# Cross attention in a decoder layer: dividing the probabilities before they are turned, and adding the outputs by channel

## The chip, the cores and the metric

One core of a Trainium2 chip runs the whole program. The time is device microseconds of one execution. The kernel before took 2195.38 us (median of three runs, 2195.28 to 2197.44). The engines are TensorE (PE in the rows; PEld is its weight loading), VectorE (DVE), ScalarE (ACT), GpSimd (POOL) and SyncE (SP), which issues the transfers. Each runs its own instructions in order, and they wait for one another by semaphores.

## The reference, cut to what matters

Three parts follow one another, each added to its input and normalized: a gated long convolution with its multilayer part, the attention, and a low rank feed-forward part. The change lies in the attention, over 16 batches of 512 tokens with 16 heads of 16 channels. The context has 64 tokens:

```python
y = jnp.einsum('bhqk,bhkd->bhqd', jax.nn.softmax(att, axis=-1), v)          # causal self attention
qc = _heads(x @ Wcq + bcq)
kc = _heads(cross_input @ Wck + bck)
vc = _heads(cross_input @ Wcv + bcv)
attc = jnp.einsum('bhqd,bhkd->bhqk', qc, kc) * scale
y = y + jnp.einsum('bhqk,bhkd->bhqd', jax.nn.softmax(attc, axis=-1), vc)    # cross attention
y = y.transpose(0, 2, 1, 3).reshape(x.shape[0], T, C)
return y @ Wp + bp
```

All of it is in float32; products are of split numbers (a high and a low part, three products) or of float32 as it is.

## The kernel before

The attention stage (`attend`) runs one step for each batch, and two steps ahead of the first. A step has 44 slots. In each slot TensorE does up to four things in this order: the weights of one unit of self attention (`weights`, 40 units, each then exponentiated by ScalarE into `pt` and masked on its diagonal by GpSimd, the "cut"), the jobs that the table `SLOTS` names for the slot, the value products of a chunk two slots behind its last unit (`outputs`, in slots 5, 11, 15, 21, 25, 31, 35 and 41), the turning of a head group's output (`turn_out`, in slots 13, 23, 33 and 43), and one piece of the next batch's scores (`scores`), whose maxima VectorE takes (L1743). Two banks hold scores and two hold weights, so that TensorE can be at most two slots ahead of VectorE's maxima and of ScalarE's exponentials. The jobs share three PSUM banks, `ps_j`, in turn.

Jobs are named by a letter and a number: c is the cross query, kc and vc are the context's keys and values, v the values, t the turning of the input, q and k the self attention's queries and keys, n the turned maxima, y the turning of the output, p the output projection. Each step works on several batches: q, k and t two ahead, c, s, w, o and r one ahead, y and p one behind. The cross attention is four kinds of job:

- s (8 jobs, L1666 and L1669 on VectorE): scores of 128 tokens by 8 heads x 64 context tokens. VectorE takes the maximum of each head and writes the scores less the maximum into `sd`. There is one `sd` for each quarter of the tokens, so s4 waits until w3 has read it.
- w (8 jobs, L1346, L1480): a head pair's shifted scores of all 512 tokens are turned (four transpositions of 128x128), and ScalarE takes their exponential into `ptc`.
- o (4 jobs, L1352, L1483): two head pairs' values times `ptc`. The values carry a column of ones for each head, which gives the sum of its exponentials, and are 32 columns a head wide (`VW`), so one pair makes 64 output rows. ScalarE copies the result to `sc`.
- r (4 jobs, L1357, L1677, L1679): `sc` is turned back to tokens by channels (four transpositions), and VectorE divides by the sum and writes into `y`.

`divide` then does the same for the self attention's output and adds it to `y` (L1704, L1706, L1710). The jobs y0 and y1 of the next step turn `y` to channels by tokens (L1361), and it is split in a high part (ScalarE, L1487) and a low part (VectorE, L1683) for the projection.

Other work of GpSimd in a step: `low_part` (L1559) in the slots of q and k (9, 11, 17, 19), `context_keys` (L1573) in slots 3 to 6, the layer norm's root (`ln_root`, L1579 to L1585) in slot 16 and the residual addition (L1589) in slot 37. The order of all of it is written out by hand in the code of each engine's `step` and in the table.

## Time and profile before

| | |
|---|---|
| median of three runs | 2195.38 us |
| profiled execution | 2197.36 us |
| its span | 2195.6 us |
| TensorE busy over the span | 1985.4 us, 90% |
| VectorE | 1468.2 us, 67% |
| ScalarE | 1222.3 us, 56% |
| GpSimd | 883.2 us, 40% |
| mean granted clock of TensorE | 0.965 of full speed |

The page has these shares, and a strip of forty slices. In that strip the attention stage is the long middle part, where TensorE is at nine tenths or more in every slice and its clock is at full speed. The timeline gives the instructions of one engine in order of time, with the idle time ahead of each and who ended it. Views by stretches give the busy time of each engine between two moments.

### The profile page before, as it was taken

To read this page: it belongs to the slowest core of one execution; us is meant where nothing else is said; L and a number is where in the kernel's file an instruction comes from. 1 tells how busy PE (TensorE), PEld (TensorE's weight loads), DVE (VectorE), ACT (ScalarE), POOL (GpSimd) and SP (SyncE) were. 2 spreads that over 40 slices of the span, in tenths; PEclk is the share of its full clock that TensorE was granted. 3 is DMA by queue.
4 is the path that set the end of the run, shared out by engine and by line. 5 is a ranking of instruction groups with operands and counts; after the bars stand their busy time and mean duration, and the time that the engine had idled before them with its cause. 6 is when DMAs were issued, how large, how long until landed. Compare 5 with 4: busy or idle time off the path is not lost. (4 is left out here: it accounts for less than half of the span.)

```text
span 2195.6 us, 39396 instructions
## 1 busy us (share of the span) xinstructions
PE 1985.4 (90%) x12897; PEld 1348.4 (61%) x12960; DVE 1468.2 (67%) x2652; ACT 1222.3 (56%) x2425; POOL 883.2 (40%) x1336
## 2 busy tenths in 40 slices
PE   6786949999999868999999999999999999968997
PEld 4665337888888755566566665566655665535554
DVE  6898634555555427777778777777777787724776
ACT  6775535555555423665656656565656556645554
POOL 3443615555555431334333434344333433332222
PEclk9999969999999979999999999999999999978999
DMA  3343121211122244343443344342443334112221
GB/s 116 123 149 125 44 77 68 77 68 69 67 73 76 78 106 91 77 106 72 104 105 85 79 93 103 92 103 64 109 103 80 90 81 94 43 39 66 78 87 66
DMA packets 104787, 188.10 MB, mean 86 GB/s; under 512 B 27961, under 2 KB 78137, under 8 KB 98489
## 3 DMA queue, kind: packets, MB, share of 16 engines
q1 hardware_dynamic: 104632, 186.13, 31.7%
q8 instruction: 86, 1.41, 0.3%
q14 instruction: 69, 0.56, 0.1%
HBM read 110.23 MB, written 58.79 MB: 77 GB/s over the span
## 5 line engine op out<-in xcount | busy, mean ns | idle before, releaser
L1516 ACT ACTIVATE at_pt<-at_ps_w 128x512 f32<-128x512 f32 x640 | 377.8, 598 | 232.8 <-PE at_ps_w L1392 232.7
L1743 DVE TENSOR_REDUCE at_mneg<-at_ps_s 128x1 f32<-128x384 f32 (+3 forms) x704 | 437.3, 636 | 94.9 <-PE at_ps_s L1381 87.3
L1606 POOL TENSOR_SCALAR_AFFINE_SELECT at_pt<-at_pt 128x256 f32<-128x256 f32 (+1 forms) x640 | 233.5, 368 | 576.3 <-ACT at_pt L1516 573.8
L1380 PE MATMUL at_ps_s<-at_ks,at_qs 96*128 96x128 bf16 (+3 forms) x1024 | 259.4, 306 | 25.0 <-DVE at_mneg L1743 22.7
L1392 PE MATMUL at_ps_w<-at_qs,at_ks 97*128 97x512 bf16 (+3 forms) x1024 | 244.3, 301 | 9.0 <-ACT at_pt L1516 5.0
L1380 PEld LDWEIGHTS at_ps_s<-at_ks,at_qs 96*128 96x128 bf16 x1024 | 86.2, 99 | 215.1 <-DVE at_mneg L1743 140.5
L895 POOL TENSOR_TENSOR ml_m_lo<-ml_m,ml_m_hi 128x512 fp32r<-128x512 f32 x80 | 115.9, 1450 | 181.0 <-ACT ml_m_hi L801 180.7
L1408 PE MATMUL at_ps_o<-at_pt,at_val 128*32 128x512 f32 (+3 forms) x2048 | 169.1, 449 | 9.7 <-POOL at_pt L1606 9.5
L1381 PE MATMUL at_ps_s<-at_mask,at_ident 128*128 128x128 bf16 (+1 forms) x641 | 149.4, 233 | 0.0
L834 ACT ACTIVATE ml_gl<-ml_ps_g 128x512 f32<-128x512 f32 x96 | 56.7, 591 | 153.8 <-PE ml_ps_u L127 150.0
L1392 PEld LDWEIGHTS at_ps_w<-at_qs,at_ks 97*128 97x128 bf16 x1024 | 88.3, 98 | 62.9 <-ACT at_pt L1516 14.8
L1559 POOL TENSOR_TENSOR at_parts<-at_rest,at_parts 128x512 bf16<-128x512 f32 x64 | 74.4, 1163 | 130.4 <-ACT at_parts L1493 130.4
L125 PE MATMUL ml_ps_o<-gw_wd,ml_m_hi 128*128 128x256 f32 x320 | 91.8, 287 | 12.8 <-POOL ml_rest L900 7.0
L1022 DVE TENSOR_TENSOR ml_m<-ml_gl,ml_ps_u 128x512 f32<-128x512 f32 x80 | 54.7, 683 | 72.7 <-POOL ml_rest L900 42.0
L381 ACT ACTIVATE pj_zc<-pj_ps_z,pj_tb,pj_tap 128x512 f32<-128x512 f32 x96 | 74.5, 780 | 47.0 <-PE pj_ps_z L127 46.9
L1666 DVE TENSOR_REDUCE at_mcneg<-at_ps_j 128x8 f32<-128x512 f32 x128 | 87.7, 685 | 17.3 <-PE at_ps_j L127 17.2
L1911 ACT ACTIVATE ff_hid<-ff_ps_h,fw_bias 128x512 f32<-128x512 f32 x128 | 79.3, 687 | 35.5 <-PE ff_ps_h L1843 34.2
L1669 DVE TENSOR_TENSOR at_sd<-at_ps_j,at_mcneg 128x512 f32<-128x512 f32 x128 | 88.6, 692 | 13.5 <-DVE at_mcneg L1666 0.5
L1002 DVE TENSOR_TENSOR ml_r<-ml_ps_o,ml_xy 128x1024 f32<-128x1024 f32 x16 | 19.6, 1225 | 116.3 <-PE ml_ps_o L943 116.3
L125 PE MATMUL at_ps_j<-at_x_hi,ea_w_hi 128*128 128x512 f32 x192 | 90.8, 473 | 6.7 <-DVE at_rest L1647 5.2
L125 PE MATMUL pj_ps_z<-pj_x_hi,pj_w_hi 128*128 128x512 f32 x192 | 80.2, 418 | 15.2 <-DVE pj_x_lo L483 15.2
L1408 PEld LDWEIGHTS at_ps_o<-at_pt,at_val 128*32 128x32 f32 x2048 | 51.9, 111 | 66.3 <-issue 44.3
(255 smaller groups left out, 5582.3 us busy)
## 6 DMA issues: line engine op xcount, KB each, us to landing
parts_d<-at_parts SPq DMA_DIRECT2D x64, 384.0 KB, 2.5
at_ks<-parts_d SPq DMA_DIRECT2D x192, 128.0 KB, 7.8
at_qs<-parts_d SPq DMA_DIRECT2D x32, 384.0 KB, 5.7
pj_xin<-in_x SPq DMA_DIRECT2D x16, 512.0 KB, 5.3
gate_d<-pj_zc SPq DMA_DIRECT2D x16, 512.0 KB, 2.7
xv_all<-pj_turned_xv SPq DMA_DIRECT2D x16, 512.0 KB, 4.2
ml_turned_y<-xv_all SPq DMA_DIRECT2D x16, 512.0 KB, 3.4
ml_x<-gate_d SPq DMA_DIRECT2D x16, 512.0 KB, 4.3
```

Of the source, the lines that this page charges most:

```text
L125: pe.matmul(out, lh, rh, start=first and k == 0, stop=False)
L895: pool.tensor_tensor(m_lo[slot(k, par)][:], m[k % 2][:], m_hi[slot(k, par)][:].bitcast(F32), ALU.subtract).then_inc(m_low, 1)
L1380: pe.matmul(out[:, i, :], qs[par][0:ROWS, h, toks], ks[par][0:ROWS, h, 0:(qt + 1) * P], start=i == 0, stop=False)
L1381: pe.matmul(out[:, :, toks], ident16[:], mask16[:, 0:count, :], start=False, stop=True).then_inc(scored, 1)
L1392: mm = pe.matmul(bank[:, at0:at0 + T - kt * P], ks[par][:, h, kt * P:(kt + 1) * P], qs[par][:, h, kt * P:T], start=True, stop=True)
L1408: mm = pe.matmul(ps_o[j * VW:(j + 1) * VW, kt * P:T], val[par][:, kt, g * HG + j, :], pt[unit % RING][:, at0:at0 + T - kt * P], start=kt = ...
L1516: act.activation(pt[u % RING][:], ps_w[u % 2][:], ACT.Exp, scale=SCALE).then_inc(exped, 1)
L1606: pool.affine_select(out=diag, in_=diag, compare_op=ALU.is_ge, fill=0.0, base=0, pattern=pattern, channel_multiplier=-1).then_inc(cut, 1)
L1666: dve.tensor_reduce(top, scored_c, AX_X, ALU.max, negate=True).then_inc(mc_set, 1)
L1669: dve.tensor_tensor(sd[qt][:].rearrange("p (e s) -> p e s", s=CL), scored_c, top.unsqueeze(2).to_broadcast([P, HE, CL]), ALU.add).then_inc ...
L1743: dve.tensor_reduce(mneg[:, g, h0 % HG:h0 % HG + count, qt], view_score(ps_s[s % 2], qt, count), AX_X, ALU.max, negate=True).then_inc(maxe ...
L1911: act.activation(hid[k % RING][:], ps_h[k % RING][:], ACT.Gelu_apprx_tanh, bias=bias1[:, k:k + 1]).then_inc(gelu_done, 1)
```

## The change

The probabilities are divided while they still lie as tokens by context. Two slots after an s job ScalarE takes the exponential of `sd` in place. Four slots after it VectorE sums the exponentials of each head and takes the reciprocal (`cross_share`), and GpSimd multiplies `sd` by it (`cross_scale`). The w jobs turn finished probabilities, and ScalarE only copies them. An o job now takes four head pairs with 32 columns each, so two o jobs do what four did, and their output is by channel: there are no r jobs, and no `sc`. ScalarE keeps the outputs in `yc`. `y` holds self attention alone; `divide` has no addition. The jobs y turn it, VectorE adds the turned bank to `yc`, ScalarE makes the high part and GpSimd the low part. In the table vc is in slot 18 and the w jobs are in slots 22 to 25 and 39 to 42, the s jobs of the second half in 26 to 32. Ahead of the stage, SyncE clears the seven semaphores of the long convolution at the end of the multilayer part.

```diff
-SLOTS = """c0 c1 kc v0,n3 v1 t0 t1 y0 y1 q0 s0 k0 s1 p0 s2 p1 s3,n0 q1 w0 k1 vc w1 w2 w3,o0 n1,s4 r0 o1 s5 r1
-           s6 - s7 - - w4 w5 w6,o2 w7 r2,o3 n2 r3 - - -""".split()
+SLOTS = """c0 c1 kc v0,n3 v1 t0 t1 y0 y1 q0 s0 k0 s1 p0 s2 p1 s3,n0 q1 vc k1 - - w0 w1 n1,w2 w3 s4 - s5 o0 s6 - s7
+           - - - - - - n2,w4 w5 w6 w7 o1""".split()
...
+            for semaphore in spent:
+                sp.sem_clear(semaphore)
...
                 elif kind == "w":
                     k, own = i // QT, slice(i % QT * P, (i % QT + 1) * P)
-                    cleared([f"s{QT * k + q}" for q in range(QT)], name, b)
+                    pe.wait_ge(cross_scaled, KT * QT * b + QT * (k + 1))
...
-                    for a in range(2):
-                        mm = pe.matmul(bank[a * 2 * VW:(a + 1) * 2 * VW, :], valc[:, 2 * i + a].rearrange("p a v -> p (a v)"),
-                                       ptc[:, (2 * i + a) % (HE // 2), :], start=True, stop=True)
-                elif kind == "r":
-                    cleared([f"o{i}"], name, b)
-                    for q in range(QT):
-                        mm = pe.transpose(bank[:, q * P:(q + 1) * P], sc[:, q * P:(q + 1) * P], ident[:])
+                    for a in range(QT):
+                        mm = pe.matmul(bank[a * 2 * HD:(a + 1) * 2 * HD, :], valc[:, QT * i + a].rearrange("p a v -> p (a v)"),
+                                       ptc[:, a, :], start=True, stop=True)
...
-                    act.activation(ptc[:, i % (HE // 2), :], bank[:], ACT.Exp, scale=SCALE).then_inc(clear(name, b)[0], 1)
+                    act.activation(ptc[:, i % QT, :], bank[:], ACT.Copy).then_inc(clear(name, b)[0], 1)
...
+            def cross_exp(name, b):
+                act.wait_ge(*clear(name, b))
+                qt = int(name[1]) % QT
+                act.activation(sd[qt][:], sd[qt][:], ACT.Exp, scale=SCALE).then_inc(cross_exped, 1)
...
+                    for name in crossed(b, u, 2):
+                        cross_exp(name, b + 1)
...
+            def cross_scale(name, b):
+                number = KT * QT * b + int(name[1])
+                pool.wait_ge(cross_shared, number + 1)
+                qt = int(name[1]) % QT
+                scores = sd[qt][:].rearrange("p (e s) -> p e s", s=CL)
+                pool.tensor_tensor(scores, scores, shares[int(name[1]) % 2][:].unsqueeze(2).to_broadcast([P, HE, CL]),
+                                   ALU.mult).then_inc(cross_scaled, 1)
+
+            def output_low(name, b, npar):
+                i = int(name[1])
+                pool.wait_ge(y_high, 2 * b + i + 1)
+                pool.tensor_tensor(yt_lo[:, i, :], yc[npar][:, i, :], yt_hi[:, i, :].bitcast(F32), ALU.subtract).then_inc(y_low, 1)
...
-                elif kind == "r":
-                    dve.wait_ge(front_ready, at(name, b))
-                    src = bank[:].rearrange("p (q h v) -> p q h v", h=HG, v=VW)
...
-                    dve.reciprocal(rdenc[:], src[:, :, :, HD]).then_inc(rdenc_set, 1)
-                    dve.wait_ge(rdenc_set, NG * b + i + 1)
-                    dve.tensor_tensor(y[npar][:, :, i * HG:(i + 1) * HG, :], src[:, :, :, 0:HD],
-                                      rdenc[:].unsqueeze(3).to_broadcast([P, QT, HG, HD]), ALU.mult).then_inc(done, 1)
                 elif kind == "y":
-                    dve.wait_ge(y_high, 2 * b + i + 1)
-                    dve.tensor_tensor(yt_lo[:, i, :], bank[:], yt_hi[:, i, :].bitcast(F32), ALU.subtract).then_inc(done, 1)
+                    dve.wait_ge(tail_ready, at(name, b))
+                    dve.wait_ge(*clear("o%d" % i, b))
+                    dve.tensor_tensor(yc[npar][:, i, :], bank[:], yc[npar][:, i, :], ALU.add).then_inc(done, 1)
...
+            def cross_share(name, b):
+                i = int(name[1])
+                number = KT * QT * b + i
+                dve.wait_ge(cross_exped, number + 1)
+                sums = mcneg[:, i % QT, i // QT * HE:(i // QT + 1) * HE]
+                dve.tensor_reduce(sums, sd[i % QT][:].rearrange("p (e s) -> p e s", s=CL), AX_X, ALU.add).then_inc(cross_summed, 1)
+                dve.wait_ge(cross_summed, number + 1)
+                wait(dve, cross_scaled, number - 1)
+                dve.reciprocal(shares[i % 2][:], sums).then_inc(cross_shared, 1)
...
-                own = y[par][:, :, g * HG:(g + 1) * HG, :]
-                dve.tensor_tensor(own, own, ys[:], ALU.add).then_inc(y_added, 1)
+                dve.tensor_tensor(y[:, :, g * HG:(g + 1) * HG, :], src[:, :, :, 0:HD],
+                                  rden[:].unsqueeze(3).to_broadcast([P, QT, HG, HD]), ALU.mult).then_inc(y_set, 1)
...
+                    for name in crossed(b, u, 4):
+                        cross_share(name, b + 1)
```

The helper `crossed(b, u, later)` names the s jobs of the slot `later` slots back. On VectorE and on GpSimd its work stands at the end of the slot: on VectorE behind the slot's maximum, on GpSimd behind the slot's cut and low part and ahead of context keys, root and residual.

GpSimd, slots 13 to 20 of a steady step, before. AFFINE_SELECT is the cut of a unit, `at_parts` the low part, the four rows from `at_lnv` to `at_mv` the layer norm's root:

```order
L1606 AFFINE_SELECT at_pt<-at_pt 128x2x128 x3
L1579 TENSOR_SCALAR at_lnv<-at_mv 128x4
L1580 TENSOR_SCALAR at_mv<-at_mv 128x4
L1583 TENSOR_TENSOR at_lnr<-at_lnv,at_mhalf 128x4
L1585 TENSOR_TENSOR at_mv<-at_mv,at_lnr 128x4
L1606 AFFINE_SELECT at_pt<-at_pt 128x2x128
L1559 TENSOR_TENSOR at_parts<-at_rest,at_parts 128x512
L1606 AFFINE_SELECT at_pt<-at_pt 128x2x128 x2
L1559 TENSOR_TENSOR at_parts<-at_rest,at_parts 128x512
```

And now, from the multiplication for s1 in slot 16 on:

```order
L1602 TENSOR_TENSOR at_sd<-at_sd,at_shares 128x512
L1589 TENSOR_SCALAR at_lnv<-at_mv 128x4
L1590 TENSOR_SCALAR at_mv<-at_mv 128x4
L1593 TENSOR_TENSOR at_lnr<-at_lnv,at_mhalf 128x4
L1595 TENSOR_TENSOR at_mv<-at_mv,at_lnr 128x4
L1629 AFFINE_SELECT at_pt<-at_pt 128x2x128
L1569 TENSOR_TENSOR at_parts<-at_rest,at_parts 128x512
L1629 AFFINE_SELECT at_pt<-at_pt 128x2x128
L1602 TENSOR_TENSOR at_sd<-at_sd,at_shares 128x512
L1629 AFFINE_SELECT at_pt<-at_pt 128x2x128
L1569 TENSOR_TENSOR at_parts<-at_rest,at_parts 128x512
L1629 AFFINE_SELECT at_pt<-at_pt 128x128
```

A multiplication of `sd` stands ahead of the root and between the cuts of units 18 and 19; the value product of slot 21 needs the cut of unit 19.

VectorE, from slot 16's s3 on, before. `at_mneg` are the maxima of self attention, `at_rest` the work of q1 and k1:

```order
L1666 TENSOR_REDUCE at_mcneg<-at_ps_j 128x8
L1669 TENSOR_TENSOR at_sd<-at_ps_j,at_mcneg 128x512
L1743 TENSOR_REDUCE at_mneg<-at_ps_s 128x1
L1647 SCALAR_TENSOR_TENSOR at_rest<-at_ps_j,ea_bias,at_parts 128x512
L1743 TENSOR_REDUCE at_mneg<-at_ps_s 128x1 x2
L1647 SCALAR_TENSOR_TENSOR at_rest<-at_ps_j,ea_bias,at_parts 128x512
L1743 TENSOR_REDUCE at_mneg<-at_ps_s 128x1
```

And now:

```order
L1696 TENSOR_REDUCE at_mcneg<-at_ps_j 128x8
L1699 TENSOR_TENSOR at_sd<-at_ps_j,at_mcneg 128x512
L1773 TENSOR_REDUCE at_mneg<-at_ps_s 128x1
L1726 TENSOR_REDUCE at_mcneg<-at_sd 128x8
L1729 RECIPROCAL at_shares<-at_mcneg 128x8
L1676 SCALAR_TENSOR_TENSOR at_rest<-at_ps_j,ea_bias,at_parts 128x512
L1773 TENSOR_REDUCE at_mneg<-at_ps_s 128x1
L1670 TENSOR_TENSOR at_valc<-at_ps_j,ea_brow 64x8x16 x2
L1773 TENSOR_REDUCE at_mneg<-at_ps_s 128x1
L1726 TENSOR_REDUCE at_mcneg<-at_sd 128x8
L1729 RECIPROCAL at_shares<-at_mcneg 128x8
L1676 SCALAR_TENSOR_TENSOR at_rest<-at_ps_j,ea_bias,at_parts 128x512
```

The sums and reciprocals of s1 and s2 stand behind the maxima of slots 16 and 18, and the context's values (vc) have moved up between them.

TensorE, slot 23, before: `at_sd` is a w job, `at_ptc` an o job, `at_so` turn_out:

```order
L1346 MATMUL at_ps_j<-ea_ident,at_sd 128x128 x4
L1352 MATMUL at_ps_j<-at_ptc,at_valc 64x512 x2
L1416 MATMUL at_ps_o<-ea_ident,at_so 128x128 x4
L1380 MATMUL at_ps_s<-at_ks,at_qs 128x256 x2
L1381 MATMUL at_ps_s<-at_mask,at_ident 128x2x128
```

And now:

```order
L1356 MATMUL at_ps_j<-ea_ident,at_sd 128x128 x4
L1422 MATMUL at_ps_o<-ea_ident,at_so 128x128 x4
L1386 MATMUL at_ps_s<-at_ks,at_qs 128x256 x2
L1387 MATMUL at_ps_s<-at_mask,at_ident 128x2x128
```

These are the rows of slot 23. The o job has left it, and its w job is now w1, where it was w3.

## Rows read from the trace of the kernel before

**Rows 1.** Stretches: us, then busy us and count by engine, TensorE's clock.

```profile
1216.20:1286.40 70.20, 67.84 (x513) 43.32 (x516) 54.31 (x107) 42.12 (x81) 27.31 (x54) 1.00 0.40 92
...
1100.00:1900.00 800.00, 770.61 (x5809) 490.08 (x5854) 620.02 (x1216) 477.98 (x919) 307.12 (x616) 1.00 0.38 89
```

**Rows 2.** TensorE's timeline, an o job and an r job: start, us, instruction.

```profile
1207.29 1.08 PE L1352 MATMUL at_ps_j<-at_ptc,at_valc 128*64 128x512 f32 x4
1208.30 0.34 PE L1380 MATMUL at_ps_s<-at_ks,at_qs 96*128 96x384 bf16 x1
...
1209.64 0.60 PE L1357 MATMUL at_ps_j<-ea_ident,at_sc 128*128 128x128 f32 x4
1210.17 1.08 PE L1352 MATMUL at_ps_j<-at_ptc,at_valc 128*64 128x512 f32 x4
```

**Rows 3.** TensorE's timeline from out3 to slot 26.

```profile
1252.94 1.50 PE L1408 MATMUL at_ps_o<-at_pt,at_val 128*32 128x384 f32 x24
...
1254.99 0.61 PE L1346 MATMUL at_ps_j<-ea_ident,at_sd 128*128 128x128 f32 x4
1255.43 0.39 PE L1380 MATMUL at_ps_s<-at_ks,at_qs 96*128 96x128 bf16 x4
...
1259.63 0.50 PE L125 MATMUL at_ps_j<-at_km_hi,at_cq_hi 128*128 128x512 f32 x1 [0.67 <-ACT at_ptc L1480]
...
1260.44 0.40 PE L1380 MATMUL at_ps_s<-at_ks,at_qs 96*128 96x256 bf16 x2
...
1261.54 1.07 PE L1408 MATMUL at_ps_o<-at_pt,at_val 128*32 128x512 f32 x8
...
1262.77 0.38 PE L1392 MATMUL at_ps_w<-at_qs,at_ks 97*128 97x384 bf16 x2
```

**Rows 4.** VectorE's timeline, slots 12 to 18.

```profile
1237.97 0.69 DVE L1666 TENSOR_REDUCE at_mcneg<-at_ps_j 128x8 f32<-128x512 f32 x1 [0.23 <-PE at_ps_j L127]
1238.76 0.69 DVE L1669 TENSOR_TENSOR at_sd<-at_ps_j,at_mcneg 128x512 f32<-128x512 f32 x1
...
1240.85 0.42 DVE L1706 TENSOR_TENSOR at_ys<-at_ps_o,at_rden 128x256 f32<-128x256 f32 x1
1241.31 0.42 DVE L1710 TENSOR_TENSOR at_y<-at_y,at_ys 128x256 f32<-128x256 f32 x1
...
1248.38 0.55 DVE L1743 TENSOR_REDUCE at_mneg<-at_ps_s 128x1 f32<-128x384 f32 x1
1248.84 0.74 DVE L1647 SCALAR_TENSOR_TENSOR at_rest<-at_ps_j,ea_bias,at_parts 128x512 f32<-128x512 f32 x1
1249.50 1.15 DVE L1743 TENSOR_REDUCE at_mneg<-at_ps_s 128x1 f32<-128x384 f32 x2
```

**Rows 5.** GpSimd's timeline, slots 16 to 18.

```profile
1246.81 0.20 POOL L1579 TENSOR_SCALAR at_lnv<-at_mv 128x4 f32<-128x4 f32 x1 [0.53 <-DVE at_mv L1698]
...
1248.62 0.41 POOL L1606 TENSOR_SCALAR_AFFINE_SELECT at_pt<-at_pt 128x256 f32<-128x256 f32 x1
1250.33 1.16 POOL L1559 TENSOR_TENSOR at_parts<-at_rest,at_parts 128x512 bf16<-128x512 f32 x1 [1.31 <-ACT at_parts L1493]
1251.44 0.84 POOL L1606 TENSOR_SCALAR_AFFINE_SELECT at_pt<-at_pt 128x256 f32<-128x256 f32 x2
```

**Rows 6.** Line L1573 by tile: count, ns min/median/max, first and last start.

```profile
L1573 POOL TENSOR_TENSOR at_km_hi<-at_kc_hi,ea_heads x32: 1043/1044/1047, 807.6 to 1856.9; 128x512 fp32r<-128x512 f32 x32
```

**Rows 7.** GpSimd's timeline at the end of the step.

```profile
1280.27 2.36 POOL L1589 TENSOR_TENSOR at_r<-at_r,ea_brow 128x1024 f32<-128x1024 f32 x1
1282.58 0.78 POOL L1606 TENSOR_SCALAR_AFFINE_SELECT at_pt<-at_pt 128x256 f32<-128x256 f32 x2
```

**Rows 8.** TensorE's timeline there: the value product of slot 41.

```profile
1283.41 1.50 PE L1408 MATMUL at_ps_o<-at_pt,at_val 128*32 128x384 f32 x24 [0.28 <-POOL at_pt L1606]
```

**Rows 9.** Stretches of step -1, columns as in rows 1.

```profile
848.00:859.40 11.40, 7.11 (x39) 3.49 (x41) 10.69 (x21) 0.60 (x1) 0.00 (x0) 1.00 0.61 88
859.40:862.90 3.50, 3.50 (x18) 2.58 (x17) 2.69 (x5) 0.60 (x1) 0.00 (x0) 0.51 0.00 0
```

More of the change, by code:

```diff
@@ L1123, in attend @@
         ptc = n.sb("ptc", [P, HE // 2, T])
[L1124 removed]
+        valc = n.sb("valc", [P, HE, 2, HD])
         so = n.sb("so", [P, T])
[L1126 to L1129 removed]
+        shares = [n.sb(f"shares{i}", [P, HE]) for i in range(2)]
+        rden = n.sb("rden", [P, QT, HG])
+        y = n.sb("y", [P, QT, H, HD])
+        yc = [n.sb(f"yc{i}", [P, KT, T]) for i in range(2)]
         yt_hi, yt_lo = n.sb("yt_hi", [P, KT, T], F32R), n.sb("yt_lo", [P, KT, T], F32R)
@@ L1160, in attend @@
         PARS = early.pars
-        CONSTS = 9
+        CONSTS = 7
         def at(job, b):
@@ L1185, in slots, with crossed @@
                 yield u, [j for j in names if shown(j, b)]
+        def crossed(b, u, later):
+            names = SLOTS[u - later] if u >= later else []
+            return [j for j in names if j[0] == "s" and shown(j, b)]
         def before(job, b):
@@ L1529, in _ @@
             for name in TAIL:
-                job(name, B - 1)
+                job(name, B - 1, 1)
             for q in range(QT):
@@ L1617, in _ @@
             over_steps(pool, step)
+            for name in ("y0", "y1"):
+                output_low(name, B - 1, 1)
             ln_root(B - 1)
```

77 lines of the change are left out of this document (37 added, 40 removed).

## The prediction

> **What bounds the kernel now.** I read the page's busy shares first, then the stage by stretches, then the timeline of one steady step, engine by engine. The change touches the attention stage alone (and adds seven semaphore clears on SyncE at the end of the stage before it). That stage runs one step per batch, 14 of them alike. The one that I read, from the start of its c0 job to the next one's, is 1216.2 to 1286.4, 70.2 us; in it TensorE is busy 67.8 us, VectorE 54.3, ScalarE 42.1, GpSimd 27.3, at full clock, as in all 800 us around it [rows 1]. So TensorE bounds the step, and what leaves its stream should be gained, as long as nobody is late for it. TensorE is in order, and the reader is to see in rows 3 to 5 and 7 how near the others already come: the transposition w3 is waited for through its exponential (0.67 us before s4 [rows 3]), and the last value product of the step waits 0.28 us for GpSimd's masking, which stands behind a 2.36 us addition there [rows 7, 8].
>
> I call slots by their number: 44 in a step, about 1.6 us each. "out3" is the value product of slot 21, "out7" that of slot 41.
>
> **TensorE's saving.** Gone are four r jobs (0.53 us each from 1209.64 to 1210.17 [rows 2]) and half of the eight o pairs' time: an o job took 1.01 us for two heads' pairs (1207.29 to 1208.30 [rows 2]), with 64 output columns each. The new one has four products of 32 columns. The value product of slot 25 has that form, four of 32 columns and 512 elements, and takes 1.07 us from its first start to its last end [rows 3], where the o job of two took 1.08 [rows 2]. So two o jobs now cost 2.0 for 4.0. Together 2.1 + 2.0 = 4.1 us a step.
>
> **VectorE's change.** Gone: four divisions r (reciprocal and multiplication), four additions L1710. An instruction starts some 0.08 before the end of an independent one (1248.38 + 0.55 against 1248.84, 0.74 before 1249.50) and some 0.1 after one that it needs (1237.97 + 0.69 against 1238.76 [rows 4]). So the addition takes 0.46 off (1240.85 to 1241.31 [rows 4]), an r about 0.6. Added: eight shares, each a sum over 128x512 (0.79 until its reciprocal may start, as L1666 to L1669) and a reciprocal of 8 columns, for which I take 0.17 from its larger sister (0.25 less the overlap; between 0.1 and 0.25): 0.96 each. Net 7.7 - 1.8 - 2.5 = +3.4 us. Throughput is not exceeded (57.7 of 66). Where it stands is what counts.
>
> **ScalarE.** Four copies of sc go, two copies o and eight exponentials come, some 0.5 each: +3 us on 42, two slots ahead of need. I cost it at nothing; the cover is its 28 us of idle time in a step.
>
> **GpSimd.** Added: eight multiplications of 128x512. No such row exists. The nearest has two inputs, one broadcast: 1.044 us [rows 6]; the addition of rows 7 does 1024 elements in 2.36, so 1.18 for 512. I take 1.10. Also two subtractions y at the same price, in slots 7 and 8, where no value product is near; nothing. The trouble is that GpSimd runs in order, and the masking ("cut") of each unit, which the value products wait for, now queues behind a multiplication that itself waits for VectorE.
> The Trainium skill ("GPSIMD Engine Reference", Engine selection) holds against two-input work on GpSimd that it is about twice as slow as VectorE. Against VectorE's 0.69 the rows above say 1.5 to 1.7 times; by the rule a multiplication would be 1.38 and the step 0.8 us longer, since three stand on the path below, 12 us in all. The rows decide.
>
> **First place: out3.** VectorE is without a pause from 1237.97 to 1250.65, the end of slot 18, in the trace (13 rows more lie between those shown [rows 4]). Its slot 16 ended with the reduction before 1248.84. Add s0's share (0.96), take off the addition (0.46), and add s1's share until its end (0.79 + 0.25): 1250.38. From there GpSimd is one queue: handover 0.15 (an estimate; 0.05 between rows 7 and 8), multiplication 1.10, the layer norm's root 1.81 (1246.81 to 1248.62), cut 0.41, the low part 1.11 (1250.33 to 1251.44 [rows 5]), cut 0.41, multiplication 1.10, the cut of unit 19 0.41, handover 0.05: out3 starts at 1256.93 where it started at 1252.94 [rows 3]. **+4.0**. TensorE, with w0 and w1 gone from ahead of it, stands idle for most of 4 us.
>
> **From out3 to slot 26.** Before: 1252.94 to 1262.77, 9.83 us [rows 3]. Gone: o0 1.01, s4 with its wait 0.67 + 0.81, r0 0.45 (0.53 less a change of tile shape that stays, some 0.08). Added: two transpositions of 0.44 (1254.99 to 1255.43), and w0's wait for s3's multiplication: GpSimd needs 1.11 + 0.31 + 1.10 + 0.05 after the cut, TensorE 2.05, so 0.5. Sum 8.24: slot 26 starts at 1265.2, **+2.4** against before.
>
> **Second place: slots 26 to 39.** TensorE has only four s, one o and the small work here, some 13 us; VectorE is the longer. It starts 1.2 after the slot does (s4 0.81: 1259.63 to 1260.44 [rows 3]; 0.2 each, as estimates, for the unit's scores ahead of it and for the end of the last product) and then has, until s7's share is done: four s of 1.40 (0.79 + 0.61), four shares of 0.96 (the last with 0.25 whole), one division 0.62, four reductions of 384 at 0.46, seven of 512 at 0.60 = 16.2 us: 1282.6. GpSimd then: 0.15, multiplication 1.10, cut 0.41, the residual addition 2.31 (1280.27 to 1282.58 [rows 7]), two cuts 0.82, 0.05: out7 at 1287.4, before 1283.41 [rows 8]. Meanwhile w4, w5 and w6 fit in.
>
> **To the end of the step.** Before 2.99 (1283.41 to 1286.4 [rows 1, 8]). Now w7 (0.44), o1 (1.01) and o1's wait for the copy of w7 (0.60 of ScalarE and two handovers less a score of 0.3, so 0.57) are in it: 5.01. The step ends at 1292.4: **+6.0 us**, in which TensorE's 4.1 are already counted.
>
> **The clock.** Before, TensorE is at full clock in the steady stretch [rows 1]. Where it was busy 7.11 of 11.40 us, its clock then stood at 0.51 for 3.5 us [rows 9], that is the lower of its two levels, 1.2 GHz. A pause of 4 us at out3, with smaller ones ahead of it, leaves TensorE idler than that. I expect one such fall a step, right before out3, w0 to w3 and out4, where TensorE is the bound: 3.4 us of work at half speed lose 1.7 us. Bounds: nothing, and two falls, 3.4.
> The Trainium skill ("TensorE: Matmul & The Clock Gate", Part 1) has the gate go to half rate after an idle stretch; rows 9 agree. Without it the sum would be the second case below.
>
> **Sum.** 14 steady steps (batches 1 to 14): 14 x 6.0 = 84.0. Step 0 has no layer norm root: 6.0 - 1.8 = 4.2. Step -1 is VectorE's (10.69 us busy of 11.40 [rows 9]); it gains up to 7.7 - 2.5 = 5.2 of its work, between 0 and that I take 4. The last step has no cross attention: 0. Clock 14 x 1.7 = 23.8. The clears: seven SyncE instructions beside a block's end, under 1 us, nothing. Together +116.0 on the span of 2195.6 = 2311.6, and 1.8 around it (2197.36 - 2195.6): 2313.4. The profiled execution lies 0.1% above the median of 2195.38, so I leave it at that: **2313 us**.
>
> **Rivals.**
> (a) The forecast: waits at GpSimd's queue, and the clock falls with them. Chance 0.50.
> (b) The waits without the falls: 2290. For it: the value products and transpositions around the pauses are dense. Against: rows 9. Chance 0.23.
> (c) The waits are half as long (+3 us a step, few falls), about 2240. VectorE's chain would have to be some 3 us looser at both places, for instance if sums from SBUF are quicker than from PSUM. Against: 12.7 us without a gap in rows 4's stretch. Chance 0.15.
> (d) The other side: TensorE stays the bound and the 4.1 us are gained in 15 steps, 2197.4 - 61.5 = 2136. Mechanism: cut 19 and s7's share come in time. It decides where out3's cut is ready by 1252.1 (its old start less w0 and w1's transpositions), that is if the 6.55 us of GpSimd's queue were under 1.7. No row of it can shrink so. It needs VectorE to run ahead as well. Chance 0.06.
> (e) Two falls a step, or multiplications of 1.4 us: 2340 to 2365. Chance 0.06.
> That the outputs by channel do not save TensorE time at all (32 columns cost as 64) would add 2.0 a step only where TensorE bounds; it is within (a).
>
> **How the numbers follow.** 2313 is that of (a); its own range, with 0.5 to 1.5 falls and 5 to 7 us a step, is 2285 to 2335. For 8 in 10 I take in (b), the upper part of (c) and the lower of (e): 2250 to 2350. A difference of 0.2% (4.4 us) is what a measurement tells. Faster: (d), 0.06. Within: the edge between (c) and (d), 0.02. Slower: 0.92.
>
> **What would show it.** Right: a steady step of 76 to 79 us; TensorE's longest waits on L1414 (out3, out6, out7) for GpSimd's cut, and on L1356 (w0, w4) for the multiplication; granted clock under 1.00 in the steady stretch; GpSimd without a pause from s1's multiplication to cut 20. o jobs of four products in 1.0 us. Wrong: no wait over 1 us at L1414, or a step under 70 us. The sum is wrong in size if the multiplication is not 1.05 to 1.2, or a share not about 0.96.

## The result, and the profile after

The changed kernel takes **2301.01 us** (median of 4 runs, 2300.68 to 2303.87), the kernel before 2195.33 (4 runs on the same chip): ratio **1.048** (95% interval 1.046 to 1.050), slower. The forecast was 2313 in a range of 2250 to 2350. The profiled execution took 2301.33, with a span of 2299.6, 104.0 us more than before's.

Counted between the starts of the first and the last residual addition of the stage, 15 steps apart, a step of after takes 74.43 us on average and one of before 68.26 (first and last start are 938.7 and 2055.2, and 929.4 and 1953.3 before). Among batches 1 to 14 alone, from c0 to c0, it is 76.53 against 70.22 (948.45 to 1943.32 and 937.34 to 1850.21, 13 intervals each): **+6.3 us a step**. Step -1 gave 6.3 more, step 0 5.3, and the time from the last c0 to the end of the program 10.9, in which the last full step's 6.3 are contained.

Stretches of after, columns as in [rows 1]: a steady step, two parts of it, and the long stretch.

```profile
1330.50:1407.00 76.50, 66.33 (x499) 42.01 (x502) 56.90 (x113) 45.87 (x88) 37.33 (x64) 0.98 0.37 85
...
1367.50:1370.70 3.20, 0.09 (x5) 0.03 (x4) 2.86 (x6) 2.38 (x6) 3.20 (x6) 1.00 0.27 94
1370.70:1374.20 3.50, 3.50 (x27) 1.45 (x28) 0.11 (x1) 1.13 (x3) 2.56 (x4) 0.51 0.42 140
...
1100.00:1900.00 800.00, 700.38 (x5188) 445.88 (x5229) 593.12 (x1160) 478.77 (x911) 390.71 (x669) 0.96 0.36 83
```

The reader is to compare the last row with the last of [rows 1]: TensorE was busy 771 of 800 us and is now busy 700, though part of it ran at a lower clock; no other engine is near its limit (VectorE 593, GpSimd 391). Nobody became the bound as a total. The time is in pauses, and the rows in the middle are one of them: 3.2 us in which TensorE did 0.09 us of work while GpSimd worked without a gap, and behind it 3.5 us at 0.51 of the clock, the lower of the two levels.

TensorE's timeline of that step, whose c0 starts at 1330.51 and the next one's at 1406.44 (start, us, instruction, in brackets its idle time and whom it waited for), beside [rows 3, 8]:

```profile
1370.68 2.73 PE L1414 MATMUL at_ps_o<-at_pt,at_val 128*32 128x384 f32 x24 [3.11 <-POOL at_pt L1629]
...
1379.64 0.38 PE L1398 MATMUL at_ps_w<-at_qs,at_ks 97*128 97x384 bf16 x2
...
1393.48 1.06 PE L1414 MATMUL at_ps_o<-at_pt,at_val 128*32 128x512 f32 x8 [1.48 <-POOL at_pt L1629]
...
1398.28 0.63 PE L1356 MATMUL at_ps_j<-ea_ident,at_sd 128*128 128x128 f32 x4 [1.32 <-POOL at_sd L1602]
...
1401.59 1.50 PE L1414 MATMUL at_ps_o<-at_pt,at_val 128*32 128x384 f32 x24 [1.29 <-POOL at_pt L1629]
...
1404.65 1.07 PE L1362 MATMUL at_ps_j<-at_ptc,at_valc 128*32 128x512 f32 x8 [0.46 <-issue]
...
1406.41 0.38 PE L1398 MATMUL at_ps_w<-at_qs,at_ks 97*128 97x512 bf16 x1
```

Four waits for GpSimd stand where before had one of 0.28 us: out3 (3.11), out6 (1.48), w4 (1.32) and out7 (1.29). The first row also shows the clock: 24 products that took 1.50 us in [rows 3] take 2.73 here.

This step is one of the two shortest of steps 1 to 13 (75.9 us, the average is 76.5), and in its clock it isn't typical. Read stretch by stretch, after has 24 stretches of 3.5 us at the lower level in these 13 steps, 6.4 us a step; before has none in them. Only this step and one other have a single one. Eleven have two: in six of them the two adjoin, from some 2 us ahead of out3 to 5 us behind it, and in five the second comes 24 to 27 us later, at out6 or w4. A whole step of the first kind, and pieces out of the two stretches of a step of the second kind:

```profile
1100.41:1177.05 76.64, 66.47 (x498) 42.09 (x500) 56.37 (x111) 45.89 (x87) 37.34 (x64) 0.96 0.37 85
...
1217.25:1220.50 3.25, 2.93 (x25) 1.12 (x26) 0.15 (x1) 0.81 (x3) 2.90 (x5) 0.50 0.49 165
1241.25:1244.50 3.25, 3.25 (x17) 2.09 (x17) 2.37 (x6) 1.51 (x3) 1.94 (x4) 0.50 0.00 0
```

GpSimd's timeline ahead of out3 and ahead of out7, beside [rows 5, 7]:

```profile
1364.42 1.05 POOL L1602 TENSOR_TENSOR at_sd<-at_sd,at_shares 128x512 f32<-128x512 f32 x1 [3.75 <-DVE at_shares L1729]
1365.55 0.20 POOL L1589 TENSOR_SCALAR at_lnv<-at_mv 128x4 f32<-128x4 f32 x1
...
1367.36 0.41 POOL L1629 TENSOR_SCALAR_AFFINE_SELECT at_pt<-at_pt 128x256 f32<-128x256 f32 x1
1367.74 1.16 POOL L1569 TENSOR_TENSOR at_parts<-at_rest,at_parts 128x512 bf16<-128x512 f32 x1
1368.84 0.41 POOL L1629 TENSOR_SCALAR_AFFINE_SELECT at_pt<-at_pt 128x256 f32<-128x256 f32 x1
1369.22 1.04 POOL L1602 TENSOR_TENSOR at_sd<-at_sd,at_shares 128x512 f32<-128x512 f32 x1
1370.21 0.41 POOL L1629 TENSOR_SCALAR_AFFINE_SELECT at_pt<-at_pt 128x256 f32<-128x256 f32 x1
...
1397.09 1.04 POOL L1602 TENSOR_TENSOR at_sd<-at_sd,at_shares 128x512 f32<-128x512 f32 x1 [0.57 <-ACT at_pt L1528]
...
1398.46 2.35 POOL L1612 TENSOR_TENSOR at_r<-at_r,ea_brow 128x1024 f32<-128x1024 f32 x1
1400.77 0.77 POOL L1629 TENSOR_SCALAR_AFFINE_SELECT at_pt<-at_pt 128x256 f32<-128x256 f32 x2
```

The first row is s1's multiplication, which had to wait 3.75 us for VectorE's share. From there to the cut of unit 19 (1370.21 to 1370.62) GpSimd has no gap: multiplication, root, cut, low part, cut, multiplication, cut. Below the second "..." is the queue ahead of out7, with the residual addition in the middle.

VectorE's timeline where s1's share is made, beside [rows 4]:

```profile
1363.42 0.68 DVE L1726 TENSOR_REDUCE at_mcneg<-at_sd 128x8 f32<-128x512 f32 x1
1364.13 0.20 DVE L1729 RECIPROCAL at_shares<-at_mcneg 128x8 f32<-128x8 f32 x1
1364.25 0.71 DVE L1676 SCALAR_TENSOR_TENSOR at_rest<-at_ps_j,ea_bias,at_parts 128x512 f32<-128x512 f32 x1
```

And the lines of the page that hold most of the waits: count, busy us, mean ns, idle time before them and its releaser.

```profile
L1414 PE MATMUL at_ps_o<-at_pt,at_val 128*32 128x512 f32 (+3 forms) x2048 | 186.3, 488 | 93.0 <-POOL at_pt L1629 92.8
L1602 POOL TENSOR_TENSOR at_sd<-at_sd,at_shares 128x512 f32<-128x512 f32 x128 | 133.7, 1045 | 214.3 <-DVE at_shares L1729 208.6
L1356 PE MATMUL at_ps_j<-ea_ident,at_sd 128*128 128x128 f32 x512 | 83.9, 291 | 18.9 <-POOL at_sd L1602 18.9
```

In these, 93 us of TensorE's idle time is the value products' wait for GpSimd's cut and 19 us the transpositions' wait for the multiplication: 112 us over 16 steps, 7.0 each. The other part is the clock: 6.4 us a step at half speed make TensorE's own work 3.2 us longer. 7.0, less the 0.3 that before had, and 3.2 make 9.9, and with the 4.1 that left TensorE's stream some 5.8 of the 6.3.

### The profile page after: what moved, and what is told of

Same layout as the page of the kernel before. It is cut to its first block and busy times, and to the rows that moved or that the text cites. A ratio compares the mean times of both kernels' runs of the same rounds, so it can differ in the third digit from the quotient of the medians.

```text
span 2299.6 us, 39230 instructions
## 1 busy us (share of the span) xinstructions
PE 1963.2 (85%) x12641; PEld 1327.7 (58%) x12704; DVE 1502.5 (65%) x2716; ACT 1281.4 (56%) x2521; POOL 1043.2 (45%) x1494
## 5 line engine op out<-in xcount | busy, mean ns | idle before, releaser
L1528 ACT ACTIVATE at_pt<-at_ps_w 128x512 f32<-128x512 f32 x640 | 371.9, 593 | 196.1 <-PE at_ps_w L1398 190.7
L1386 PE MATMUL at_ps_s<-at_ks,at_qs 96*128 96x128 bf16 (+3 forms) x1024 | 270.2, 316 | 38.5 <-DVE at_mneg L1773 34.1
L1414 PE MATMUL at_ps_o<-at_pt,at_val 128*32 128x512 f32 (+3 forms) x2048 | 186.3, 488 | 93.0 <-POOL at_pt L1629 92.8
L1398 PE MATMUL at_ps_w<-at_qs,at_ks 97*128 97x512 bf16 (+3 forms) x1024 | 249.7, 306 | 14.7 <-ACT at_pt L1528 10.3
L1602 POOL TENSOR_TENSOR at_sd<-at_sd,at_shares 128x512 f32<-128x512 f32 x128 | 133.7, 1045 | 214.3 <-DVE at_shares L1729 208.6
L1414 PEld LDWEIGHTS at_ps_o<-at_pt,at_val 128*32 128x32 f32 x2048 | 56.9, 119 | 157.5 <-POOL at_pt L1629 112.9
L1398 PEld LDWEIGHTS at_ps_w<-at_qs,at_ks 97*128 97x128 bf16 x1024 | 90.7, 101 | 75.2 <-issue 20.1
L1356 PE MATMUL at_ps_j<-ea_ident,at_sd 128*128 128x128 f32 x512 | 83.9, 291 | 18.9 <-POOL at_sd L1602 18.9
L1569 POOL TENSOR_TENSOR at_parts<-at_rest,at_parts 128x512 bf16<-128x512 f32 x64 | 74.4, 1162 | 53.6 <-ACT at_parts L1505 53.5
```

What stands on the lines that cost most here:

```text
L1356: mm = pe.transpose(bank[:, q * P:(q + 1) * P], sd[q][:, own], ident[:])
L1386: pe.matmul(out[:, i, :], qs[par][0:ROWS, h, toks], ks[par][0:ROWS, h, 0:(qt + 1) * P], start=i == 0, stop=False)
L1398: mm = pe.matmul(bank[:, at0:at0 + T - kt * P], ks[par][:, h, kt * P:(kt + 1) * P], qs[par][:, h, kt * P:T], start=True, stop=True)
L1414: mm = pe.matmul(ps_o[j * VW:(j + 1) * VW, kt * P:T], val[par][:, kt, g * HG + j, :], pt[unit % RING][:, at0:at0 + T - kt * P], start=kt = ...
L1528: act.activation(pt[u % RING][:], ps_w[u % 2][:], ACT.Exp, scale=SCALE).then_inc(exped, 1)
L1602: pool.tensor_tensor(scores, scores, shares[int(name[1]) % 2][:].unsqueeze(2).to_broadcast([P, HE, CL]), ALU.mult).then_inc(cross_scaled, 1)
```

## The experiments

All ratios are against the kernel before, run on the same chip at the same time; 4 runs each where nothing else is said. The theory A of each expectation is the prediction's: GpSimd's queue, and VectorE ahead of it, make TensorE wait at two places, and the clock falls there. Theories C and D, in e4 and e5, are about what the falls cost.

**e1, the root out of the queue ahead of out3.** The layer norm's root (slot 16) is issued in slot 21, and ScalarE's four normalizations come five slots later with it (in slots 24 to 27).

```
+ROOT_SLOT = 21
-                    if 0 <= u - P1_SLOT - 4 < QT and shown("p1", b):
-                        layernorm(b - 1, u - P1_SLOT - 4)
+                    if 0 <= u - ROOT_SLOT - 3 < QT and shown("p1", b):
+                        layernorm(b - 1, u - ROOT_SLOT - 3)
-                    if u == P1_SLOT + 1 and shown("p1", b):
+                    if u == ROOT_SLOT and shown("p1", b):
```

> The changed kernel with one thing moved: the layer norm's root on GpSimd from slot 16 (behind the multiplication for s1) to slot 21 (behind that slot's cut), and ScalarE's four normalizations with it, to slots 24 to 27. Nothing else. Theory A (GpSimd's queue sets the start of out3): the root's 1.81 us leave the queue between s1's multiplication and cut 19, TensorE's wait at out3 falls from 3.1 us to about 1.3 to 1.6, each of 14 steps is 1.5 to 1.8 us shorter, total 2270 to 2280. Rival B (VectorE's own chain sets it, and GpSimd's cut is only the last that is seen): the share for s2 is late too, the root filled a time in which GpSimd would wait anyway, total 2296 to 2301.

**e2, the residual addition out of the queue ahead of out7.**

```
-                    if u == NU - 3 and back(b):
+                    if u == NU - 1 and back(b):
```

> The changed kernel with GpSimd's residual addition moved from slot 37 (ahead of the cuts 38 and 39) to slot 39, behind its cut. Nothing else. Theory A: cut 39 comes 2.3 us earlier, out7 waits no longer (1.29 us in the trace) and o1 follows; a step is 1.3 to 2.0 us shorter, total 2270 to 2282. Rival B (w4 to w7, which wait for the last multiplication, set the end of the step): at most 0.3 us a step, total 2296 or more.

**e3, both.** The edits of e1 and e2.

> Both moves together: root to slot 21 and residual addition to slot 39. Theory A: two separate places on one chain, so the gains add up: 2240 to 2258, with still some 1.5 us of waits at out3, out6 and w4 each step, and a result that stays above the kernel before (2195). Rival B: the second place absorbs what the first gives back, total no lower than the better of the two alone, some 2270.

Measured: e1 2277.47 us (ratio 1.037, 1.035 to 1.039), e2 2279.44 (1.038, 1.037 to 1.040), e3 2255.65 (1.028, 1.026 to 1.031). So 23.5, 21.6 and 45.4 us against after: each inside A's range, and additive. Two jobs that the change did not touch, 1.81 and 2.31 us long, were worth 1.7 and 1.5 us in each of 14 steps (the total by 14, with what it changed in the clock) because of where they stood. The two places are two separate causes, and neither hides behind the other. TensorE's waits for the cut within 1100 to 1900 us (line, releaser, us in all, times, longest), of after, e1, e2 and e3:

```profile
PE at_ps_o L1414 <- POOL at_pt L1629: 57.5, 29, 3.1
```

```profile
PE at_ps_o L1415 <- POOL at_pt L1630: 43.9, 30, 1.6
```

```profile
PE at_ps_o L1414 <- POOL at_pt L1629: 48.8, 21, 3.1
```

```profile
PE at_ps_o L1415 <- POOL at_pt L1630: 33.7, 22, 1.6
```

The longest wait is halved by e1 and untouched by e2, as it should be if 3.1 is out3's; in e2 it is the number of waits that shrinks, from 29 to 21.

**e4, TensorE kept busy ahead of out3.** Ten products are added whose results nobody reads, to see what the fallen clock costs by itself.

```
+                    if back(b) and u in (21,) and shown("c0", b):
+                        pe.wait_ge(exped, NU * b + u)
+                        for _ in range(10):
+                            pe.matmul(ps_w[(u + 1) % 2][:], ident16[:], mask16[:]...)
                     outputs(...)
```

> The changed kernel with ten further products of 512 columns (bfloat16, about 2.2 us at full clock) on TensorE right ahead of out3 in each step that has cross attention, into a weight bank that is free then. They lie in the pause of 3.1 us. Theory C (the pauses cost a fall of the clock on top of themselves): out3 takes 1.5 us again instead of 2.7, half-speed stretches at that place go, and the total falls by 10 to 25 us, to 2276 to 2291. Rival D (the half-speed stretches lie where TensorE is not the bound, or the falls come from other pauses): total 2299 to 2315, since part of the added work is not hidden.

Measured: 2335.41 us (1.064, 1.062 to 1.066), in neither range. TensorE's timeline says why:

```profile
1383.86 4.02 PE L1440 MATMUL at_ps_w<-at_mask,at_ident 128*128 128x512 bf16 x10 [2.61 <-ACT at_pt L1532]
1387.81 0.95 PE L1414 MATMUL at_ps_o<-at_pt,at_val 128*32 128x384 f32 x11
```

The added products stood in a bank that is free only after ScalarE's exponential of the unit before. So they waited 2.61 us, the pause remained, and they themselves ran at half speed (4.02 us for what takes 2.33 in e5 below) and pushed out3 back. The experiment was misplaced and says nothing of the price that it was made for. It does show that the work behind the pause ran slowly here too, though it was other work.

**e5, the same ten products where nothing has to be waited for,** at the start of slot 21's weights, in the bank that they are about to overwrite.

```
                 wait(pe, exped, NU * b + u - 1)
+                if u == 21 and shown("c0", b):
+                    for _ in range(10):
+                        pe.matmul(bank[:], ident16[:], mask16[:]...)
```

> As the run before with added products, but these ten now stand at the start of slot 21, ahead of its weights, where the bank that they write is free at once; in the last one they waited 2.6 us for an exponential of ScalarE and so filled nothing of the pause. They should start with the pause and fill 2.2 of its 3.1 us. Theory C (the pause costs a fall of the clock on top of itself): the product at out3 takes 1.5 us where it took 2.7, total 2276 to 2291. Rival D (the half-speed stretch costs nothing, or falls elsewhere instead): 2297 to 2306.

Measured: 2283.41 us (1.040, 1.037 to 1.043), in C's range. **With 2.3 us of useless work added to each step the kernel is 17.6 us quicker**, 1.3 us a step over 14 steps. TensorE's timeline, and two whole steps, without and with a fall:

```profile
1359.35 2.33 PE L1398 MATMUL at_ps_w<-at_mask,at_ident 128*128 128x512 bf16 x10
...
1362.84 1.50 PE L1417 MATMUL at_ps_o<-at_pt,at_val 128*32 128x384 f32 x24 [0.94 <-POOL at_pt L1632]
...
1365.32 0.63 PE L1356 MATMUL at_ps_j<-ea_ident,at_sd 128*128 128x128 f32 x4 [0.38 <-POOL at_sd L1605]
```

```profile
1247.82:1322.67 74.85, 66.69 (x511) 41.83 (x510) 56.39 (x111) 45.82 (x87) 37.26 (x64) 1.00 0.37 87
1322.67:1397.82 75.15, 68.27 (x511) 42.97 (x510) 56.39 (x111) 45.81 (x87) 37.24 (x64) 0.98 0.37 86
```

Out3 is back at 1.50 us and the mean clock from 1100 to 1900 us at 0.99 (0.96 in after). It starts where it started in after, 40.2 us into the step, so nothing of the gain comes from ahead of it. The Trainium skill ("TensorE: Matmul & The Clock Gate", Part 1) names idleness ahead as what brings the gate down; this pair of kernels agrees: the only edit puts work into the pause, and out3 runs at full speed again.

The 1.3 us are not the whole price, since e5 still has a stretch at half speed in nine of steps 1 to 13, each at w4. A step with one takes 75.1 us. Of the four without one, two take 74.9 and two 75.2, these with another wait in them. After's average is 76.5, so its falls cost some 1.6 us a step together. The price of one depends on where it lies: 0.3 at w4, and 1.1 at out3 with a single stretch (out3 to slot 26 takes 8.96 us in the step shown above, 7.90 in e5).

**e6, the multiplication made small:** it multiplies one of a head's 64 context tokens alone, so the output is not the reference's.

```
-                pool.tensor_tensor(scores, scores, shares[...][:].unsqueeze(2).to_broadcast([P, HE, CL]),
+                pool.tensor_tensor(scores[:, :, 0:1], scores[:, :, 0:1], shares[...][:].unsqueeze(2),
```

> The changed kernel with GpSimd's multiplication done for the first of each head's 64 context tokens alone (8 columns of 512), so its result isn't the reference's; waits and order are kept. Theory A: each multiplication falls from 1.04 to about 0.15 us. Two of them stand ahead of out3, one each ahead of out6, w4 and out7: 3 to 3.6 us a step less and fewer clock falls, total 2238 to 2256. Rival B (VectorE's sums are the price): at most 1 us a step, 2285 or more.

**e7, the sum made small too:** it goes over 4 of the 64 tokens. VectorE and GpSimd then have next to nothing of the change's added work, TensorE has all of its savings.

```
-                dve.tensor_reduce(sums, sd[...].rearrange("p (e s) -> p e s", s=CL), AX_X, ALU.add)
+                dve.tensor_reduce(sums, sd[...].rearrange("p (e s) -> p e s", s=CL)[:, :, 0:4], AX_X, ALU.add)
```

> As the last one, and VectorE's sum also takes only 4 of each head's 64 tokens, so that both added chains are nearly gone, with order and waits kept (not the reference's result). Theory A in its narrow form (all of the loss is the two additions, and what is left is TensorE's stream with 4.1 us less): total 2136 to 2150. Theory A2 (the additions cost 6 us a step, but the table and the root and the residual addition still hold TensorE, so its saving is not gained): 2180 to 2200.

Measured: e6 2233.98 (1.017, 1.014 to 1.020), 67.0 us under after and a little more than A's range gave it; e7 2194.18 (10 runs; 0.9988, 0.9977 to 0.9999), another 39.8, in the range of A2. So the multiplications cost some 4.8 us of each of 14 steps and the sums 2.8, in this order of taking them away, and both together (106.8 us) are the whole loss. The falls are in these figures: of the 24 stretches at half speed in steps 1 to 13, three are left in e6 and four in e7. e6 also has the price of a fall with no other wait to hide in, 1.3 us, from two of its steps:

```profile
1583.76:1655.12 71.36, 64.40 (x501) 40.98 (x500) 56.25 (x111) 45.43 (x87) 30.66 (x64) 1.00 0.39 91
1655.12:1727.76 72.64, 65.70 (x502) 41.40 (x500) 56.26 (x111) 45.54 (x87) 30.66 (x64) 0.98 0.38 89
```

The two are not more than the loss: **with the added work all but gone the kernel stands where it stood before, and most of TensorE's 4.1 us a step are still not gained.** From c0 to c0 a step of e7 takes 69.5 us on average, 0.7 less than before's 70.2, and the ends of the stage are some 6 us longer. Where the rest went is in TensorE's waits within 1100 to 1900 us:

```profile
PE at_ps_o L1414 <- POOL at_pt L1629: 35.2, 36, 1.5
...
PE at_ps_s L1386 <- DVE at_mneg L1773: 13.2, 26, 0.6
```

With the smaller ones these are 54.8 us in 11.5 steps, 4.8 a step, where before had 24.9 us, 2.2 a step. The cut still stands behind the root and the residual addition, and the scores wait for VectorE's reductions (13.2 us, 9.5 in before). The work that TensorE lost had been covering these.

**e8, e3 with share and multiplication one slot earlier** (three behind the scores instead of four).

```
-                    for name in crossed(b, u, 4):
+                    for name in crossed(b, u, 3):
```

(on VectorE and on GpSimd)

> Root in slot 21 and residual addition in slot 39 as before, and VectorE's share and GpSimd's multiplication three slots behind the scores where they were four. The result is the reference's. Theory A: what is waited for at out3, w0 and w4 comes a slot earlier, 1.3 to 1.7 us a step less than with the two moves alone (2255.7), and out6, out7 with it: 2222 to 2238. Rival B (VectorE is full there, so a share done earlier only puts off the maxima that TensorE waits for): 2250 to 2258.

Measured: 2213.63 us (1.008, 1.005 to 1.011), 42.0 less than e3, below the lower end of what was expected. Its waits, same stretch, then the row of that stretch:

```profile
PE at_ps_s L1387 <- DVE at_mneg L1774: 36.8, 56, 1.4
PE at_ps_j L1334 <- DVE at_sd L1700: 16.7, 12, 1.6
PE at_ps_j L1357 <- POOL at_sd L1603: 9.0, 11, 1.1
PE at_ps_o L1415 <- POOL at_pt L1630: 5.7, 11, 1.1
```

```profile
1100.00:1900.00 800.00, 724.85 (x5611) 460.00 (x5610) 635.11 (x1251) 517.78 (x975) 417.49 (x722) 1.00 0.38 88
```

The waits for the cut have fallen from 33.7 to 5.7 us, but they have gone over to VectorE: 53.5 us on its reductions and subtractions (19.0 in e3). With the order of jobs as it is, whichever of the two small engines is relieved, the other is next. All waits together are hardly fewer, 73.4 us for 74.4. What has gone is the half speed: 20 stretches in steps 1 to 13 of e3, one in e8, and the mean clock rises from 0.96 to 1.00 (of TensorE's 800 us, 724.85 are busy, 723.01 in e3: as many, with more done in them).

**e9, another order of jobs.** The root in slot 22, the residual addition behind its cut, the share three slots behind the scores and the multiplication four, and a table with s0 to s3 one or two slots earlier (in 9, 10, 13 and 15) and most of the empty slots strewn between the jobs (the longest row of them is five, six in after).

```
-SLOTS = """c0 c1 kc v0,n3 v1 t0 t1 y0 y1 q0 s0 k0 s1 p0 s2 p1 s3,n0 q1 vc k1 - - w0 w1 n1,w2 w3 s4 - s5 o0 s6 - s7
-           - - - - - - n2,w4 w5 w6 w7 o1""".split()
+SLOTS = """- c0 c1,kc,v0 - v1,t0 t1 - y0 n3 y1,s0 s1,q0 - - s2,k0 - q1,s3 - p0,n0 - p1 - k1,w0 vc w1,w2 - w3,s4,s5 -
+           s6,n1 - - - s7,o0 - - - - - n2 - w4 w5 w6,w7 - o1""".split()
+ROOT_SLOT = 22
-                    for name in crossed(b, u, 4):
+                    for name in crossed(b, u, 3):
```

(the last on VectorE alone)

> The changed kernel with the two moves (root now in slot 22, residual addition in 39), the share three slots and the multiplication four behind the scores, and another table: the s jobs of the first half in slots 9, 10, 13 and 16 with pauses between, those of the second half begun right after w3 in slot 26, y, q and k one to two slots off, so that VectorE's long slots lie between long slots of TensorE. The result is the reference's. Theory A (the form with shares is 4.1 us a step cheaper on TensorE, and only the waits hid it): TensorE is the bound again, a step lasts 65 to 67 us, total 2110 to 2150, under the kernel before. Rival E (the saving on TensorE isn't there, products of 32 columns and the rest cost as much as before): no lower than 2185.

**e10, the kernel before with the two moves of e1 and e2 alone,** in its own lines.

```
+ROOT_SLOT = 21
-                    if u == P1_SLOT + 1 and shown("p1", b):
+                    if u == ROOT_SLOT and shown("p1", b):
-                if u == NU - 3 and back(b):
+                if u == NU - 1 and back(b):
```

> The kernel before, with only the two moves on GpSimd and ScalarE: root to slot 21, residual addition to slot 39. In its trace out7 waits 0.28 us for a cut behind that addition. Theory A: 0.3 us a step there and as much at the copies of w3, 2185 to 2193. Rival (its small pauses were part of one chain and more comes free, 1.0 to 1.5 us a step): 2172 to 2182. It tells how much of the last kernel's time is owed to the moves alone.

Measured: e9 **2129.44 us** (5 runs; 0.970, 0.968 to 0.972), in A's range and quicker than both kernels; e10 2172.26 (6 runs; 0.989, 0.987 to 0.991). So of e9's 66.8 us, 24.0 can be had by the moves in the old form of the computation as well, and the other 42.8 come with the new form and its table (and a root one slot later). The fences are e9's stretch, a step of it and its largest wait, then the same stretch and a step of e10:

```profile
1100.00:1900.00 800.00, 760.13 (x5985) 492.36 (x5983) 649.79 (x1296) 537.69 (x1051) 446.98 (x785) 0.99 0.39 93
...
1332.17:1396.78 64.61, 62.96 (x500) 41.86 (x499) 55.18 (x111) 44.10 (x87) 37.12 (x64) 1.00 0.43 105
```

```profile
PE at_ps_s L1386 <- DVE at_mneg L1773: 16.8, 22, 1.2
```

```profile
1100.00:1900.00 800.00, 781.42 (x5955) 495.69 (x5951) 625.30 (x1229) 489.36 (x939) 311.13 (x627) 1.00 0.39 90
...
1278.71:1347.65 68.94, 67.66 (x517) 43.29 (x516) 54.19 (x107) 42.26 (x81) 27.11 (x54) 1.00 0.40 94
```

A step, from the first to the last residual addition by 15, is 63.60 us in e9 (935.5 to 1889.5) and 66.86 in e10 (930.9 to 1933.8). e10 has TensorE busy 781 of 800 us: it is near the bound of the old form. e9 goes below that because its TensorE has less to do; at 760 of 800 it isn't at its own yet. The two single steps are both at full clock, and TensorE is busy 62.96 us in the one and 67.66 in the other: the saving in its work is there, 4.7 us by this pair, and e9 cashes most of it. How much of the 42.8 us the form gives and how much the table, would need the old form with a table of its own, and that was not run.

The clock in all of the kernels, steps 1 to 13: the mean step from c0 to c0, and the time in it at the lower level.

| kernel | step, us | at half speed, us a step |
|---|---|---|
| before, e10 | 70.2, 69.0 | 0, 0 |
| after | 76.5 | 6.4 |
| e1, e2, e3 | 74.7, 75.3, 73.6 | 5.1, 6.7, 5.4 |
| e4, e5 | 78.5, 75.1 | 6.4, 2.4 |
| e6, e7 | 71.7, 69.5 | 0.8, 1.1 |
| e8, e9 | 70.9, 65.3 | 0.3, 0.8 |

## Why the prediction was right

Mechanism, places and sign were right; the size was 12 us too high, on a loss of 105.7. By its steps, in us from the start of c0, with the step of the timelines above as measured, one of the two with a single fall:

| step of the prediction | predicted | measured |
|---|---|---|
| out3 starts | 40.7 | 40.2 |
| slot 26 starts | 49.0 (without the clock) | 49.1 (with it) |
| s7's multiplication starts | 66.6 | 66.6 |
| out7 starts | 71.2 | 71.1 |
| the step ends | 76.2, with the clock 77.9 | 75.9 here, 76.5 on average |

**VectorE's change.** A share was taken as 0.96 us until the next may start, 0.79 for the sum and 0.17 for the reciprocal. It took 0.83 (1363.42 to 1364.25): 0.71 until the reciprocal, and 0.12 from there. s0's and s1's shares lie ahead of s1's multiplication, which so started 0.3 to 0.4 earlier than foreseen (1364.42 is 33.9 into the step, 34.3 by the prediction); that is most of the 0.5 by which out3 came early.

**GpSimd's multiplication.** Taken 1.10, measured 1.045 (128 of them, 133.7 us). Of the two neighbours [rows 6] had the right one, the one with a broadcast operand. In the queue ahead of out3 there were two, and 0.1 us came of it.

**First place: out3.** As predicted: s1's multiplication to the cut of unit 19 without a pause, and 3.11 us of idle time. e1 took the root out and got 1.7 us a step; e6 took the multiplications' length out, here and at the second place, and got 4.8.

**From out3 to slot 26: the term that was mis-sized.** It was given 8.24 us (its own terms add up to 8.27), with 0.5 for w0's wait for s3's multiplication, and the fallen clock was put on top with 1.7. Measured are 8.96 with both (1370.68 to 1379.64), 9.3 on average. The two are not added: out3 at half speed ends at 1373.34, when s3's multiplication (1371.96 to 1373.00) is done, so w0's wait is gone. The slow clock filled a wait that was priced separately. e5 has the same stretch at full speed, and there the wait is back, 0.38 us ahead of w0: 7.90 us, 0.3 under the 8.24.

**Second place.** Right to 0.1 us in its length (66.6 - 49.1 = 17.5 against 17.6), but two things in it cancelled. The four shares were 0.13 shorter each. And out6's wait of 1.48, which the prediction gave no price of its own, came back to VectorE, which had been taken as busy without a pause: it stood idle for scores that TensorE could do only behind out6.

```profile
1395.02 1.16 DVE L1773 TENSOR_REDUCE at_mneg<-at_ps_s 128x2 f32<-128x512 f32 x2 [0.35 <-PE at_ps_s L1387]
```

Apart from this VectorE and GpSimd bind there, so the rest of out6's wait is TensorE's idle time and no addition to the step. e2 showed the residual addition's part, 1.5 us a step. w4 waited 1.32 where w4 to w6 had been said to fit in; it is again time that TensorE had.

**The clock.** The place was right, out3 above all, and the number of 1.7 us a step was near the truth, but not for its reason. It was to be one fall a step, with 3.4 us of work at half speed. There are 6.4 us of it a step, twice as much, and each costs less than was taken, since part of it fills waits: some 1.6 us a step by e5's steps without a fall. That two errors met here is luck. The waits are then some 4.7 of the step's loss, and 6.0 were predicted: 0.5 came off ahead of out3, 0.3 from there to slot 26, 0.4 behind it. Both terms together: 14 x 7.7 = 107.8 predicted, 14 x 6.3 = 88.3 measured. That would be 19 too much; the ends give 8 back: step -1 lost 6.3 (taken 4) and step 0 5.3 (4.2), and behind the last full step came another 4.6, where nothing was taken.

**TensorE's saving of 4.1.** Four products of 32 columns take 1.07 us, as taken from slot 25 in [rows 3]. That the 4.1 are there was only argued from such rows in the prediction; e9 and e10 have 4.7 between them, and a step of e7 at full clock is busy 64.28 us where one of before is busy 67.84 [rows 1], 3.6 less. e7 shows that most of them would not have been gained even with the added work gone, so rival (d), 2136, was further off than its price said: its condition named out3's cut alone, and the root, the residual addition and VectorE's reductions each stood ready behind it. e9 reaches 2129, but after all of them had been moved.

**Rivals.** (b), no falls, would have been right in the time of 2290 as nearly as (a) in its 2313, but not in the mechanism: the falls are in the trace, and e5 gets back 1.3 us a step. Its time is near because the waits were taken 1.3 us a step too long, which makes up for most of what the falls cost. (c), with VectorE's chain some 3 us looser, had a seed of truth: the shares are looser by 0.13 each, which over two on the way to out3 is a quarter of a microsecond and not 3.

## What to carry to other kernels

Where an in-order engine sends small results to the one that bounds the kernel, count what stands ahead of each of them in its queue, that is the time and not the load: GpSimd was busy 45% and cost 5% of the run. Work taken off the bounding engine is gained only if what had been hidden behind it is moved too; before making a form cheaper, list the waits that come next. Prices of two effects at one place (a wait, and a slower clock behind it) are not added: ask which of them ends last. And read the clock over many steps before one step is taken as typical: here equal steps had one or two stretches at half speed.
